# A sandwich of two routed feed-forwards around gated attention: another slot order, and rows turned by block transposes and two DMA queues

## The reference

```python
x = x + 0.5 * ffn(layernorm(x), w_router, w_fc, w_proj)
x = x + attention(layernorm(x), Wq, Wk, Wv, Wg, Ws, Wo, g_norm_weight)
x = x + 0.5 * ffn(layernorm(x), w_router, w_fc, w_proj)

def ffn(x, w_router, w_fc, w_proj):          # 2 experts, hidden size 2048
    probs = softmax(x @ w_router.T); top = argmax(probs); weight = probs[top]
    h = x @ w_fc[top].T
    a = square(where(h >= 0, h, 0.5 * h))
    return (a @ w_proj[top].T) * weight

# attention: 16 heads, DK = M = 64, DV = 128
s = clip(x @ Ws, -32, 32); z = cumlogsumexp(s); p = exp(s - z)
hk = hk * g_t + k_t p_t;  ok = q_t hk        # a recurrence over tokens, g = exp(z[t-1] - z[t])
pv = softmax(ok)
hv = hv * g_t + p_t v_t;  o = pv_t hv
o = o * rsqrt(mean(o^2) + eps) * g_norm_weight * silu(x @ Wg)
out = o @ Wo
```

## Time and profile before

| what | us |
|---|---|
| median of 3 runs (lowest, highest) | 1997.95 (1993.54, 1998.57) |
| the profiled execution, its own time | 1995.09 |
| its span, first to last instruction | 1993.4 |
| TensorE busy | 1907.1 |
| VectorE, ScalarE, GpSimd busy | 1295.6, 727.2, 275.6 |

### The profile page before, as it was taken

How to read it: one execution, slowest core, us unless ns; L and a number is a source line. 1 busy time by engine, 2 the same in 40 slices (tenths; PEclk the granted TensorE clock), 3 DMA queues, 4 the chain that set the end, 5 groups by cost and what they waited for, 6 DMA issues and landing times.

```text
span 1993.4 us, 30393 instructions
## 1 busy us (share of the span) xinstructions
PE 1907.1 (96%) x11600; PEld 1599.2 (80%) x11600; DVE 1295.6 (65%) x2543; ACT 727.2 (36%) x1368; POOL 275.6 (14%) x218
## 2 busy tenths in 40 slices
PE   2999999978999999999999999999999799999998
PEld 1888888857888888888888888888887688888886
DVE  5654546626777777777777777777778865454562
ACT  2654556634222222121222222221222355454673
POOL 3010102011011021020120210210201201010100
PEclk9999999998999999999999999999999899999999
DMA  6473446661112021121111121210201336433566
GB/s 231 131 219 120 115 144 177 191 194 71 30 35 39 18 57 24 16 56 22 28 43 30 30 42 21 55 26 15 59 12 43 127 112 204 130 105 118 168 194 187
DMA packets 189248, 181.36 MB, mean 91 GB/s; under 512 B 140336, under 2 KB 140336, under 8 KB 189104
## 3 DMA queue, kind: packets, MB, share of 16 engines
q1 hardware_dynamic: 181648, 162.09, 27.8%
q0 software_dynamic: 7456, 17.34, 4.2%
HBM read 137.40 MB, written 25.72 MB: 82 GB/s over the span
## 4 chain that ended last, share of the span: by engine, by line
PE 90%; DVE 4%; DMA 2%; ACT 2%; issue 1%; POOL 1%; SPq 0%; ACTq 0%; DVEq 0%; POOLq 0%
PE at_pj L1364 17%; PE at_pj L1338 14%; PE last_ff_ps_y L740 8%; PE last_ff_ps_h L285 8%; PE at_r L1429 8%; PE first_ff_ps_y L740 8%; PE first_ff_ps_h L285 8%; PE at_r L1508 3%; PE at_r L1496 2%; PE at_r L1413 1%; PE at_r L1460 1%; PE at_r L1530 1%; PE at_r L1472 1%; PE at_r L1501 1%; PE at_r L1465 1%
## 5 line engine op out<-in xcount | busy, mean ns | idle before, releaser
L1364 PE MATMUL at_pj<-at_w_lo,at_xT_hi 128*128 128x512 f32 x512 | 208.2, 407 | 0.0
L1364 PE MATMUL at_pj<-at_w_hi,at_xT_hi 128*128 128x512 f32 x512 | 200.5, 392 | 0.0
L1364 PE MATMUL at_pj<-at_w_hi,at_xT_lo 128*128 128x512 f32 x512 | 199.7, 390 | 0.0
L633 DVE TENSOR_TENSOR last_ff_w_lo<-last_ff_stage,last_ff_w_hi 128x1024 fp32r<-128x1024 f32 x78 | 95.5, 1225 | 113.1 <-ACT last_ff_w_hi L431 112.9
L633 DVE TENSOR_TENSOR first_ff_w_lo<-first_ff_stage,first_ff_w_hi 128x1024 fp32r<-128x1024 f32 x78 | 95.5, 1225 | 110.6 <-ACT first_ff_w_hi L431 110.4
L1338 PE MATMUL at_pj<-at_xT_hi,at_w_lo 128*128 128x512 f32 x384 | 157.5, 410 | 0.9 <-DVE at_xT_lo L1153 0.8
L1338 PE MATMUL at_pj<-at_xT_lo,at_w_hi 128*128 128x512 f32 x384 | 150.9, 393 | 0.0
L1338 PE MATMUL at_pj<-at_xT_hi,at_w_hi 128*128 128x512 f32 x384 | 150.8, 393 | 0.0
L932 POOL TENSOR_TENSOR at_w_lo<-at_stage,at_w_hi 128x1024 fp32r<-128x1024 f32 (+1 forms) x36 | 78.1, 2170 | 447.9 <-ACT at_w_hi L985 447.9
L999 ACT ACTIVATE at_v<-at_pj 128x256 f32<-128x256 f32 x128 | 49.1, 383 | 222.9 <-PE at_pj L1364 222.9
L1191 DVE TENSOR_TENSOR xres<-at_r,xres 128x512 f32<-128x512 f32 x128 | 88.5, 691 | 60.0 <-PE at_r L1429 58.9
(11 more groups left out here) (331 smaller groups left out, 4653.3 us busy)
## 6 DMA issues: line engine op xcount, KB each, us to landing
first_ff_stage<-wff SPq DMA_DIRECT2D x90, 512.0 KB, 4.1
last_ff_stage<-wff SPq DMA_DIRECT2D x90, 512.0 KB, 3.5
at_turned_ke<-at_ke_blocks SPq DMA_DIRECT2D x496, 32.0 KB, 2.0
at_stage<-watt SPq DMA_DIRECT2D x24, 512.0 KB, 4.0
at_stage<-watt SPq DMA_DIRECT2D x16, 384.0 KB, 3.4
xres<-x SPq DMA_DIRECT2D x4, 1024.0 KB, 9.9
mid_rows<-xres SPq DMA_DIRECT2D x4, 1024.0 KB
out<-xres SPq DMA_DIRECT2D x4, 1024.0 KB
```

The costliest lines, as they stand in the source:

```text
L633: dve.tensor_tensor(w_lo[:, t % RING, :], stage[:, t % RING, :], w_hi[:, t % RING, :].bitcast(F32), ALU.subtract).then_inc(w_lo_done, 1)
L1364: last = pe.matmul(PJ[(7 * k + 3 + t) % 2][:, :], x[:, kk, tok], wvg(w, kk), start=(kk == 0 and n == 0), stop=(kk == KC - 1 and n == 2))
```

## The change

1. The first feed-forward's slots are 256, 512, 512, 512, 256 and 128 rows wide (FIRST_WIDTHS); the second keeps the old ones (LAST_WIDTHS). Slot 0 is chosen after 512 tokens, slot 1 after 1536. Only group 0 is scattered ahead of slot 0; groups 1 and 2 are scattered beside it, group 3 beside slot 1. SP loads slot 1's rows at its step 12 of slot 0, behind the scatters of groups 1 and 2, and slot 2's at step 14 of slot 1.
2. The first four tiles of x are loaded one by one, with the router's rows after the second, and normalised two by two.
3. In attention's first 30 units u is laid out as (token tile, head), VectorE transposes it in squares in place, SP and ScalarE issue eight DMAs each that move the squares to at_u_moved (which has the place of the low part), and both parts are made from there in the next unit. The last two units keep the turns on TensorE.
4. project_out of the unit before moves behind the turn of ok, and the first two quarters of v and gate move ahead; VectorE's additions to the residual move behind p_out, two on either side of the scan of z.
5. GpSimd loads the weight pieces from its own queue, each right after the low part of the piece before; ScalarE's high parts change places.

```diff
+FIRST_WIDTHS = (GROUP // 2, GROUP, GROUP, GROUP, GROUP // 2, P)
+LAST_WIDTHS = (GROUP, GROUP, GROUP, GROUP // 2, GROUP // 2, P)
...
-    at_once = [g for g in steps if g < 2]
-    with_slot = [g for g in steps if g >= 2]
+    at_once = [g for g in steps if g < 1]
+    with_slot = [g for g in steps if g == 1 or g == 2]
+    last_slot = 0 if early else 1
...
-                if t == (3 if first_slot else 2) * RING:
+                if t == (HT - 2 if j == 1 and not early else 3 * RING if j == 0 else 2 * RING):
...
-                            sp.wait_ge(scattered[2], 16 * RT)
+                            for g in with_slot:
+                                sp.wait_ge(scattered[g], 16 * RT)
...
+        def move_u(queue, unit, rows):
+
+            queue.wait_ge(blocks_done, 4 * unit + 4)
+            queue.wait_ge(wo_mm, unit * UC + 1)
+            squares = u[:, :, :, :].rearrange("p c h (b i) -> p (c h) b i", b=SQUARES)
+            for a in rows:
+                for b in range(SQUARES):
+                    queue.dma_start(u_moved[b * SQUARE:(b + 1) * SQUARE, :, :, a * SQUARE:(a + 1) * SQUARE].rearrange("p c h i -> p (c h) i"),
+                                    squares[a * SQUARE:(a + 1) * SQUARE, :, b, :]).then_inc(u_landed, 16)
...
+            for unit in range(PAIRS * UNITS - 1):
+                move_blocks(unit + 1)
+                if unit < MOVED:
+                    move_u(sp, unit, range(SQUARES // 2, SQUARES))
...
+            def load(i, n, pair, piece):
+                col, width = PIECES[piece]
+                pool.wait_ge(piece_lo, i * NP + n + 4 + 1)
+                pool.dma_start(stage[:, 0:width], watt[pair, :, col:col + width]).then_inc(piece_there, 16)
...
+                    before = i * UNITS + k - 1
+                    if 0 <= before < MOVED:
+                        move_u(act, before, range(SQUARES // 2))
+                    if k == UNITS - 1 and more:
+                        hi_piece(i * (NP * 16) + 5 * 16, 3)
+                    if more:
                         e_exp(i, k + 1)
...
+                    if 0 <= before < MOVED:
+                        act.wait_ge(u_landed, (before + 1) * SQUARES * SQUARES * 16)
+                        act.wait_ge(wo_mm, before * UC + 1)
+                        for b in range(2):
+                            act.activation(u_half(uT_hi, b), u_half(u_moved, b), ACT.Copy).then_inc(u_hi, 1)
+                    if more:
+                        vg_read(i, k + 1, 0)
                     act.wait_ge(ok_shifted, count(i, k, 1, 1))
                     act.activation(ok[:, :, :], ok[:, :, :], ACT.Exp).then_inc(pv_done, 1)
...
+                    if 0 < i * UNITS + k <= MOVED:
+                        for b in range(2):
+                            dve.wait_ge(u_hi, count(i, k, 2, b - 1))
+                            dve.tensor_tensor(u_half(uT_lo, b), u_half(u_moved, b), u_half(uT_hi, b).bitcast(F32), ALU.subtract).then_inc(u_lo, 1)
...
-                    if (i, k) != (0, 0):
-                        project_out(*((i, k - 1) if k else (i - 1, UNITS - 1)))
+                    if not more:
+                        project_out(i, k - 1)
+                    if more:
+                        project_vg(i, k + 1, 0, i * NP + 1 + 8 if k == UNITS - 1 else 0)
                     pe.wait_ge(ok_scaled, count(i, k, 1, 1))
...
-                    if more:
-                        project_vg(i, k + 1, 1)
+                    if more and (i, k) != (0, 0):
+                        project_out(*((i, k - 1) if k else (i - 1, UNITS - 1)), (i, k))
...
-                    for b in range(2):
-                        pe.wait_ge(u_done, count(i, k, 2, b + 1))
+                    if i * UNITS + k >= MOVED:
+                        for b in range(2):
+                            pe.wait_ge(u_done, count(i, k, 2, b + 1))
...
+                        if i * UNITS + k < MOVED:
+                            dve.wait_ge(u_done, count(i, k, 2, b + 1))
+                            dve.transpose(u_half(u, b), u_half(u, b)).then_inc(blocks_done, 1)
```

More of the change, by code:

```diff
@@ L174, in phase_feed_forward @@
     to_row = sb("ff_to_row", [P, 2, GT], I32)
-    in_loaded = [sem(f"rt_in_loaded{i}") for i in range(TILES // RT)] if x_in is not None else []
+    in_loaded = [None] + [sem(f"rt_in_loaded{i}") for i in range(1, TILES // RT)] if x_in is not None else []
     if x_in is not None:
@@ L323, in slot_body @@
                 return
-            if not first_slot:
+            if j > 1 or early and j > 0:
                 sp.wait_ge(table_ready, KNOWN)
@@ L376, in gpsimd_program @@
             norms["normed"](pool, TILES // RT - 1)
-        if x_in is not None:
+            scatter(TILES // RT - 1)
+        else:
             for g in with_slot:
                 norm(g)
-        for g in with_slot:
-            scatter(g)
+            scatter(1)
+            scatter(2)
         def slot_body(j, width, after):
+            if j == 1 and not early:
+                norm(3)
+                scatter(3)
             for t in range(HT):
@@ L1032, in pair @@
                         q_scale(i, k + 1)
-                        e_exp(i, k + 1)
+                    before = i * UNITS + k - 1
[4 more added lines that the diff above has]
+                    if more:
+                        e_exp(i, k + 1)
+                    if k == UNITS - 2 and not last:
+                        hi_piece(i * (NP * 16) + 2 * 16, 0)
+                    if 0 <= before < MOVED:
[5 more added lines that the diff above has]
+                        vg_read(i, k + 1, 0)
+                    act.wait_ge(ok_shifted, count(i, k, 1, 1))
+                    act.activation(ok[:, :, :], ok[:, :, :], ACT.Exp).then_inc(pv_done, 1)
+                    if more:
+                        vg_read(i, k + 1, 1)
+                    if not more:
+                        act.sem_inc(behind["w_hi_done"], RING)
+                        for t in range(AHEAD):
+                            behind["first_hi"](act, t)
                     if k == 0:
@@ L1037, in pair @@
                         hi_piece(i + 1, 4)
-                    if k == UNITS - 1 and more:
-                        hi_piece(i * (NP * 16) + 9 * 16, 3)
-                    act.wait_ge(ok_shifted, count(i, k, 1, 1))
-                    act.activation(ok[:, :, :], ok[:, :, :], ACT.Exp).then_inc(pv_done, 1)
-                    if more:
-                        vg_read(i, k + 1, 0)
-                        vg_read(i, k + 1, 1)
-                    else:
-                        act.sem_inc(behind["w_hi_done"], RING)
-                        for t in range(AHEAD):
-                            behind["first_hi"](act, t)
+                    if k == UNITS - 2 and not last:
+                        hi_piece(i * (NP * 16) + 3 * 16, 1)
                     if last and k > 0:
@@ L1310, in pair @@
                         if k >= 2:
-                            early_slot(dve, step, routing, slot_table, k - 2, behind["table_ready"])
+                            early_slot(dve, step, routing, slot_table, k - 2, LAST_WIDTHS, k * UC, behind["table_ready"])
                     if more:
@@ L1362, in project_vg @@
                 for kk in range(KC):
+                    if pieces and kk % 2 == 0:
+                        pe.wait_ge(piece_lo, pieces + kk // 2)
                     for n, (w, x) in enumerate(parts):
@@ L1424, in project_out @@
                         pe.wait_ge(u_lo, count(i, k, 2, cc // 2 + 1))
+                    if cc == 1 and following is not None:
+                        pe.wait_ge(p_out, count(*following, 1, 1))
                     if cc >= 2:
```

343 lines of the change are left out of this document (189 added, 154 removed).

## The result

| | median us (lowest to highest) | ratio to before, 95% interval |
|---|---|---|
| before (5 runs beside it) | 1997.95 (1993.54 to 1998.57) | |
| after (5 runs) | 1982.98 (1982.36 to 1986.36) | 0.9939 [0.9928, 0.995] |

What follows compares the result with a forecast made beforehand. TensorE, busy 1907.1 of 1993.4 us, was taken as the bound. Terms of -12.3, +11.4, -25.2, +6.3 and +3.8 sum to -16.0 against 1995.09: 1979.1, forecast as 1980, range 1962 to 1998 (the forecast's own 1972 to 1989).

Steps and rivals of the forecast that it cites:

- Term 1: Start of first feed-forward: first slot needs 512 tokens placed, not 1024, so first large product near 31.5 us: -12.3 us.
- Term 2: First feed-forward: a narrow slot first gives half the cover for work beside it, costing +11.4 us.
- (d): Slots 0 and 1: base stores make weights 18 and 19 late and GpSimd's norm of group 3 late: together 6 us.
- (c): Slot 0: SP waits for group 2's scatter before loading slot 1's rows, so weight 12 lands late: 4 us.
- Term 3: Attention: 30 of 32 units lose TensorE's turns; 29 x 0.87 gives -25.2 us, with 3 us of cover for u.
- Rival D: Attention: transposes covered another wait, p_out at 0.2 us of slack; 0.4 us in 30 units, 1992; chance 0.24 with B.
- Term 4: Attention's weight pieces, loaded by GpSimd: piece 3 comes 0.9 us late in 7 pairs, +6.3 us.
- Term 5: Attention's last pair: moved additions delay the gates that free the bank for q, 2 x 1.9 us: +3.8 us.
- C: Attention: two queues share descriptor writing, so a ScalarE issue takes 1.2 us, not 0.72; 2021 us, chance 0.12.
- A: Cover holds everywhere: narrow first slot costs +4 us, weight pieces 0; 1966 us, chance 0.22.
- B: Narrow first slot costs +20 us, late weight pieces +14, so no change: 1995 us; chance 0.24 with Rival D.

Runs made afterwards that it cites:

- the half alone: New first feed-forward of the changed kernel with attention as in the kernel before: 1996.84 us, ratio 0.9999 to before.
- gate 2 early: Changed kernel with VectorE's third gate product ahead of its wait for the coefficients and the products u: 1975.70 us, ratio 0.9911 to before.
- one queue: Changed kernel with all 16 transfers of a unit's u issued by SyncE, none by ScalarE: 1994.73 us, ratio 0.9997 to before.
- the eighth experiment: Changed kernel, last pair's u turned by TensorE, w_out's products and adds of its units 1 and 2 in their former place: 1985.21 us, ratio 0.9946.

## Why the prediction was right, and where it was wrong

**Term 1** (-12.3): right within 1.4 us. The first large product came at 32.83 us, against the 31.5 forecast: -10.9. The steps were as told: the decision at 13.45 (13.5), the slot's rows asked for at 26.40 (25.9) and on chip at 30.39 (29.9).

**Term 2** (+11.4): the sum was right, its parts were not. Start to edge slot changed by -0.8 us (predicted -0.9), so the term measured +10.2, and the half alone is at 0.9999. I had put 55 us in slot 0 and 6 in slot 1 (d); it is 62.45 in slot 0 and nothing in slot 1. The wait in (c) is there as told, one weight asked for at 66.41, 5.91 us to land, TensorE resuming at 74.71. What (d) missed is where things stand: the statistics of the fourth group are in slot 0's last tile, ahead of slot 1's split, and the wide tiles hide the late weights entirely. The stores, which I had put in slot 1's account, kept slot 0 long once (c) was mended: with them (and the statistics, in the same edit) out of it, 54 us were left of 62. No term of mine has the granted clock, which is 0.92 in slot 0: in the same code slot 0 took 59.4 and 59.7 us where it was 1.00, so some 3 of the 7 us by which it passed 55 are the clock.

**Term 3** (-25.2): the mechanism was right, a size wrong. The cover for u held (between 540 and 1400 us the view of TensorE's waits has a single one of 0.4 us, for a weight piece). But "29 x 0.87" took the whole length of the turn as gain. It had covered the 0.2 to 0.3 us that gate 2 is late, and per unit 0.65 us was won, as the turns' return and gate 2's move show from both sides. Over 28 units (the first gained 1.06 us) this is some 19 us (27 x 0.67 + 1.06) where 24.4 were counted. Rival D had the right form, a transposition that was cover for another wait, but named p_out. I had looked for what the turn covered only in the new order's waits, not at VectorE's last product before it.

**Term 4** (+6.3): 2.3 us by the profile (912.15 less 27 units of 33.70). Piece 3's chain is as told: its load, high half and low half in the timeline of a fourth unit that began at 721.00:

```profile
725.41 0.61 POOL L993 DMA_DIRECT2D at_stage<-watt  x1 [0.30 <-POOL at_w_lo L980]
...
730.24 1.06 ACT L1042 ACTIVATE at_w_hi<-at_stage 128x1024 fp32r<-128x1024 f32 x1 [5.62 <-DMA at_stage<-watt]
...
731.39 2.40 POOL L980 TENSOR_TENSOR at_w_lo<-at_stage,at_w_hi 128x1024 fp32r<-128x1024 f32 x1 [5.36 <-ACT at_w_hi L1042]
```

The high half starts at 9.2 us of the unit and the low half ends at 12.8, against the 12.9 to 13.9 forecast: at the early bound, and the loss is 0.2 us in most pairs, 0.8 in the first. The wait of term 3 gave the chain 0.2 us as well; with gate 2 early piece 3 costs about 1.1 us a pair (33.8 to 35.1 where other units take 33.45), near the 0.9 predicted. The landing of 4.7 us, median, is in the range I had chosen from the nearest rows. The 3.2 us estimated from the Trainium skill's "DMA: Bandwidth & Descriptors", section "Anatomy of one DMA", do not fit: in the trace after no load of a weight piece landed in less than 3.4, and beside u's transfers one of 512 KB took 5.8.

**Term 5** (+3.8): right in size by the means, at least in part by luck. The profiles with the new last pair took 157.0, 154.0, 156.0, 154.0, 154.6 and 157.3 us from its first unit to the last feed-forward (after, attention alone, the statistics and the rows moved, one queue, turns back), those with the old one 149.7 and 152.8 (before, first feed-forward alone): means 155.5 and 151.3. Much of the scatter within each is the granted clock (the last w_out products took 6.67 to 8.44 us). I had named the place, "the gates that free the bank for q", and moving gate 2 took the time away (148.8). I blamed the additions' new place for it; the eighth experiment speaks against that as the sole cause. In unit 1 the wait was 1.1 us longer with the turns kept on TensorE too (38.51 us against 37.51), and the last pair as a whole was as long (157.3), so the lengthening belongs to the new order of products (or to that of the loads) and not to u's moves. Which part of it does so stays open.

**Rivals.** C is out: an issue from ScalarE takes 0.69 us beside SyncE's. With one queue the ratio is 0.9997, so the time saved in issuing was worth as much as the change's whole gain. The Trainium skill's page "DMA: Bandwidth & Descriptors", section "Issuing engines are not separate DMA queues", says that a second issuing engine saves sequencer time alone. The runs agree with it. A is out for slot 0 and nearly true for term 4. B is out.

So 1980 came close partly by luck, by errors that cancel: 5 to 6 us too much gain in the turns and 1.4 at the start, against 4 us too much loss in the pieces and 1.2 in slot 0. With the measured sizes the terms add up to about -14, where the medians give -15.0 and the two profiled executions -9.0; most of the rest is the last pair, which differs by 3 us and more between executions.

## What to carry to other kernels

Before work is taken from the engine that bounds, look at what its last cover hides: read the weight load's bracket and the other engines' last instruction ahead of the next product. The gain is the work less that wait, and an instruction that frees a bank belongs ahead of a wait for something else (here 5.6 us by the ratios for one line, most of it in the last pair). A wait for a transfer costs what stands behind it on its engine, not what uses the transfer. Under a saturated stretch of transfers a mended wait returns at the next one, until bytes are moved out of the stretch.

## What was unexpected of the hardware

After idle stretches of TensorE the granted clock fell (0.77 at 1502.5 to 1510 us, 0.82 behind slot 0's end in the kernel with rows by GpSimd, 0.76 at 1540 to 1590), and 24 products that take 5.7 us at full clock (2.4 GHz) took 7.30, part of them at 1.2 GHz. A short stall so costs more than its length, and equal code differs by 3 us between executions: the last pair 149.7 and 152.8 us, slot 0 59.4 us at a granted clock of 1.00 and 62.7 at 0.92.
